# Sending each row of a GNN and mixture-of-experts kernel to its two experts, as 128 row tiles, in place of all eight experts over every row

## What is computed

```python
src, dst = (edge_index[0], edge_index[1])
h = jnp.einsum('ni,hid->nhd', x, W)
e = jnp.einsum('ehd,hd->eh', h_src, a_src) + jnp.einsum('ehd,hd->eh', h_dst, a_dst)
e = jnp.where(e > 0, e, 0.2 * e)
e_max = jax.ops.segment_max(e, dst, num_segments=N)
...
alpha_norm = alpha / (alpha_sum[dst] + 1e-08)
msg = alpha_norm[:, :, None] * h_src
out_h = jax.ops.segment_sum(msg, dst, num_segments=N)
return out_h.reshape(N, H * D) @ W_out
```

```python
logits = tokens.astype(jnp.float32) @ router_w.astype(jnp.float32).T
probs = jax.nn.softmax(logits, axis=-1)
rw, re = jax.lax.top_k(probs, TOP_K)
...
for e in range(E):
    h = jax.nn.gelu(tokens @ w1[e] + b1[e], approximate=False)
    y = h @ w2[e] + b2[e]
    out = out + combine[:, e:e + 1] * y
```

## Time and profile before

| | us |
|---|---|
| median of 3 runs | 1542.62 |
| the runs | 1541.4, 1542.62, 2022.45 |
| span of the profiled execution | 1540.1 |
| busy in it: TensorE, VectorE, ScalarE, POOL | 1407.5, 1098.5, 980.3, 835.1 |

### The profile page before, as it was taken

One profiled execution on the slowest core, in us unless ns is written; L12 is line 12 of the kernel. 1 busy time (PEld: TensorE's weight loads), 2 busy tenths in 40 slices (PEclk: granted clock), 3 DMA queues, 4 the chain that ended last, 5 costly groups with the idle time before them and its releaser, 6 DMA issues.

```text
span 1540.1 us, 29587 instructions
## 1 busy us (share of the span) xinstructions
PE 1407.5 (91%) x7327; PEld 1141.6 (74%) x7327; DVE 1098.5 (71%) x3031; ACT 980.3 (64%) x2505; POOL 835.1 (54%) x886
## 2 busy tenths in 40 slices
PE   5925775999999999999999999999999999999998
PEld 4813454788888888888888887878787878787887
DVE  6726765677777777777777787877777777777543
ACT  3714554576767676766667676767676767676732
POOL 1347777665666666565656565656565656561000
PEclk9966867799999999999999999999999999999999
DMA  9564654434343434343434343434434343473000
GB/s 221 145 193 121 193 146 118 128 99 124 107 126 105 125 104 125 104 120 111 117 112 118 114 117 113 117 111 115 114 106 124 102 129 99 133 90 59 1 17 18
DMA packets 89788, 174.83 MB, mean 114 GB/s; under 512 B 22455, under 2 KB 56049, under 8 KB 89593
## 3 DMA queue, kind: packets, MB, share of 16 engines
q0 software_dynamic: 40448, 111.89, 28.1%
q1 hardware_dynamic: 48071, 60.77, 13.2%
q10 hardware_dynamic: 1106, 0.27, 0.1%
HBM read 159.24 MB, written 14.43 MB: 113 GB/s over the span
## 4 chain that ended last, share of the span: by engine, by line
PE 74%; issue 6%; DVE 5%; POOL 4%; ACT 4%; ACTq 1%; DMA 1%; DVEq 0%; POOLq 0%
PE agg_ps L1117 24%; PE ob L1192 20%; PE hb L1146 15%; POOL ring L740 4%; PE kbank L1079 3%; PE ob L1223 2%; PE ob L1146 2%; PE ob L1258 2%; PE ob L1198 1%; ACT acc L1336 1%; DVE ring L848 1%; PE kbank L1095 1%; ACT agg_ps L1339 1%; PE kbank L1094 1%; DVE oh L785 1%
## 5 line engine op out<-in xcount | busy, mean ns | idle before, releaser
L740 POOL DMA_INDIRECT ring<-table,srcE x832 | 803.0, 965 | 504.3 <-PE agg_ps L1117 264.8
L1117 PE MATMUL agg_ps<-ring,oh 128*128 128x260 f32 x1664 | 550.9, 424 | 19.8 <-ACT agg_ps L1339 10.3
L1336 ACT COPY acc<-agg_ps x831 | 307.7, 370 | 188.1 <-PE agg_ps L1117 120.4
L1192 PE MATMUL ob<-w_sb,hT 128*125 128x256 f32 x1600 | 408.4, 380 | 1.6
L1339 ACT COPY agg_ps<-zc 128x260 f32 x832 | 314.6, 378 | 98.6 <-ACT acc L1336 3.2
L1117 PEld LDWEIGHTS agg_ps<-ring,oh 128*128 128x128 f32 x1664 | 292.2, 199 | 86.7 <-issue 55.2
L1192 PEld LDWEIGHTS ob<-w_sb,hT 128*125 128x125 f32 x1600 | 295.8, 188 | 52.7 <-issue 9.6
L848 DVE TENSOR_TENSOR ring<-ring,kbank 128x1024 f32<-128x1024 f32 x208 | 244.7, 1213 | 50.3 <-ACT ring L1358 50.1
L1368 ACT ACTIVATE hT<-hb,b_sb 128x375 f32<-128x375 f32 (+1 forms) x272 | 154.0, 566 | 146.0 <-PE hb L1146 145.1
L983 DVE SCALAR_TENSOR_TENSOR y<-ob,cmb,y 125x256 f32<-125x256 f32 x400 | 188.9, 475 | 46.7 <-PE ob L1192 43.1
L1146 PE MATMUL hb<-xTh,w1l 128*128 128x376 f32 (+1 forms) x544 | 186.3, 423 | 0.0
(11 more groups left out here) (271 smaller groups left out, 1376.8 us busy)
## 6 DMA issues: line engine op xcount, KB each, us to landing
OT<-relb_d SPq DMA_DIRECT2D x52, 512.0 KB
ring<-table,srcE POOLq DMA_INDIRECT x832
y<-in_x_dram SPq DMA_DIRECT2D x50, 125.0 KB
out_dram<-y SPq DMA_DIRECT2D x50, 125.0 KB
table<-hrow SPq DMA_DIRECT2D x25, 227.5 KB
acc<-in_x_dram SPq DMA_DIRECT2D x2, 1568.0 KB
acc<-in_L_ffn_w_dram SPq DMA_DIRECT2D x1, 2048.0 KB, 14.3
w_sb<-in_L_ffn_w_dram SPq DMA_DIRECT2D x1, 2048.0 KB
```

What stands on the lines that cost most here:

```text
L740: pool.indirect_dma_start(out=rings[b % RING][:, k, :], out_offset=None, in_=table[:, :], in_offset=bass.IndirectOffsetOnAxis(ap=srcE[:, t ...
L1117: T.matmul(aggf[:, bass.ds(bank_of[k // 8][k % 8], ROW)], oh[:, (4 * b + q) % OHQ, k % 4, :], rings[b % RING][:, k, :], start=False, stop= ...
L1192: t = T.matmul(o[0:Q, 0:D], hT[:, e % 2, f, cols], w2_sb[:, e, f, :], start=f == 0, stop=f == KC - 1)
L1336: A.copy(accf[:, bass.ds(row_of[h][k % 8], ROW)], aggf[:, bass.ds(closed[h][k % 8], ROW)]).then_inc(S["ev"], 1)
```

## The change

The dense loop over experts goes. In its place:

- VectorE finds in `differences` and `positions` where each row of a group goes among the rows of its two experts; TensorE counts for it with nine small bf16 products. POOL scatters each block's normalised rows twice to `xr_d` in DRAM (`scatter`, six indirect DMAs a group, at slot 43 of the 48).
- The groups form four super groups of 15, 15, 12 and 8 blocks. When one is complete, `tiles_table` (some 25 VectorE instructions) says which 128 rows and which expert each tile has; the tiles are 37, 37, 31 and 23, together 128.
- Tile n has a slot tau. SyncE loads its rows (`load_tile`) and its expert's first weights (`load_w1`). TensorE transposes the rows in slot tau (`turn_rows`), multiplies in tau + 2 (`hidden`) and tau + 4 (`output`), plain float32 products; ScalarE copies and does Gelu, VectorE adds the bias (`results_out`), SyncE stores to `yr_d`. The first super group's tiles lie at slots 310 to 543, the second's at 550 to 742, the third's at 748 to 887 and the fourth's, one in each slot, at 892 to 914. The edges end with slot 831. In a slot TensorE does the row tile's work ahead of the chain step and `aggregate`.
- After a super group's last tile POOL gathers the two results of each row, block by block (`results`, two indirect DMAs a block, 551 to 593, 750 to 792, 894 to 905 and 921 to 928), into a ring of two, and VectorE weighs and adds them (`final`).
- The router is six plain float32 products in place of 18; the split of w1 at the start goes.

The diff, cut:

```diff
+    SGS = [range(0, 5), range(5, 10), range(10, 14), range(14, GROUPS)]
+    NSG = len(SGS)
+    blocks_in = [sum(size(g) for g in r) for r in SGS]
+    CAP = [(-(-n * Q // P) + 1) * P for n in blocks_in]
+    NT = [(2 * n * Q + NE * (P - 1)) // P for n in blocks_in]
+    TMAX = max(NT)
...
+            RL, RW, RX, RH, RY, RR = 6, 4, 2, 3, 3, 2
...
+            LEAD = 12
+            sg_of = {g: s for s, r in enumerate(SGS) for g in r}
+            begin = [at(r[-1], 42) + LEAD for r in SGS]
+            first_tile = [sum(NT[0:s]) for s in range(NSG + 1)]
+            tau, sg_tile = [], []
+            for s in range(NSG):
+                for i in range(NT[s]):
+                    tau.append(begin[s] + (i * (begin[s + 1] - begin[s]) // NT[s] if s + 1 < NSG else i))
...
+                    result, final = (t + 8 + 3 * j, t + 14 + 3 * j) if s + 2 < NSG else (t + 7 + j, t + 9 + j)
...
+                    def fill_ends(s):
+                        sp.wait_ge(S["tb"], s + 1)
+                        for e in range(NE):
+                            end = loads(ENG.SP, emptyI[0:1, s, e:e + 1], BASE[NSG] - P, WHY2)[0]
+                            sp.dma_start(xr_d[bass.ds(end, P), :], zero_d[:, :]).then_inc(z_st[s], 16)
+
+                    def load_tile(n):
+                        s, i = sg_tile[n]
+                        r = n % RL
+                        if i == 0:
+                            fill_ends(s)
+                            for g in SGS[s][-2:]:
+                                sp.wait_ge(xs_st[g % 2], scattered(g))
+                            sp.wait_ge(z_st[s], 16 * (NE + 1))
+                        off = loads(ENG.SP, tileI[0:1, s, 0, i:i + 1], BASE[NSG] - P, WHY2)[0]
+                        if n >= RL:
+                            sp.wait_ge(S["xt"], n - RL + 1)
+                        sp.dma_start(rows[:, r, :], xr_d[bass.ds(off, P), :]).then_inc(row_ld[r], 16)
...
+                    def load_w1(n):
+                        s, i = sg_tile[n]
+                        if n == 0:
+                            sp.wait_ge(ld_w1, 32 * KC)
+                        expert = loads(ENG.SP, tileI[0:1, s, 1, i:i + 1], (NE - 1) * P, WHY2)[0]
+                        if n >= RW:
+                            sp.wait_ge(S["gl"], 2 * (n - RW + 1))
+                        sp.dma_start(w1s[:, n % RW, :], w1_d[bass.ds(expert, P), :]).then_inc(w1_ld[n % RW], 16)
...
+                    def store_tile(n):
+                        s, i = sg_tile[n]
+                        sp.wait_ge(S["ye"], n + 1)
+                        sp.dma_start(yr_d[s][i * P:(i + 1) * P, :], ysb[:, n % RY, :]).then_inc(yr_st[n % RY], 16)
...
+                    def scatter(g):
+                        u = g % 2
+                        pool.wait_ge(S["px"], g + 1)
+                        for i in range(size(g)):
+                            for k in range(2):
+                                pool.indirect_dma_start(out=xr_d[:, :], out_offset=bass.IndirectOffsetOnAxis(ap=idx[0:Q, block_at(g) + i, k:k + 1], axis=0),
+                                                        in_=xn[0:Q, u, i, :], in_offset=None).then_inc(xs_st[u], 16)
+
+                    def results(b):
+                        s = sg_of[b // GB]
+                        if b == block_at(SGS[s][0]):
+                            for r in range(RY):
+                                pool.wait_ge(yr_st[r], 16 * len(range(r, first_tile[s + 1], RY)))
+                        if b >= RR:
+                            pool.wait_ge(S["cb"], b - RR + 1)
+                        for k in range(2):
+                            pool.indirect_dma_start(out=res[0:Q, b % RR, k, :], out_offset=None, in_=yr_d[s][:, :],
+                                                    in_offset=bass.IndirectOffsetOnAxis(ap=idy[0:Q, b, k:k + 1], axis=0)).then_inc(res_ld[b % RR], 16)
+
+                    dev_at = {at(g, 20): g for g in range(GROUPS)}
+                    scatter_at = {at(g, 43): g for g in range(GROUPS)}
...
+                    for sl in range(-BT, LAST * BT):
+                        if sl in dev_at:
+                            deviations(dev_at[sl])
+                        if sl in scatter_at:
+                            scatter(scatter_at[sl])
+                        for b in result_at.get(sl, []):
+                            results(b)
+                        if sl % 4 == 3 and sl // BT + RING < NBAT:
+                            gathers(sl // BT + RING, sl % BT // 4)
...
-                    def split_x(g, part):
-                        u, blocks = g % 2, parts(g)[part]
-                        c0, n = blocks[0] * Q, len(blocks)
-                        dve.wait_ge(S["uh"], TC(g, part))
-                        cols = lambda a: a[:, u, :, c0:c0 + n * Q].rearrange("p k (b c) -> p b k c", c=Q)
-                        v.tensor_tensor(cols(xTl), ob1[:, 0:n * KC * Q].rearrange("p (b k c) -> p b k c", k=KC, c=Q), cols(xTh),
-                                        ALU.subtract).then_inc(S["ul"], 1)
...
+                    def positions(g):
+                        n, j0 = size(g), block_at(g)
+                        dve.wait_ge(S["ps"], g + 1)
+                        p_, o1, o2 = place_[0:Q, 0:n, :], one1[0:Q, 0:n, :], one2[0:Q, 0:n, :]
+                        link(v.tensor_tensor(p_, ob[0:Q, 0:n * NE].rearrange("p (b e) -> p b e", e=NE),
+                                             carry[0:Q, :].unsqueeze(1).to_broadcast([Q, n, NE]), ALU.add))
+                        pair_(v.tensor_tensor(at1[0:Q, 0:n, :], o1, p_, ALU.mult),
+                              v.tensor_tensor(at2[0:Q, 0:n, :], o2, p_, ALU.mult))
+                        pair_(v.tensor_reduce(spot[0:Q, j0:j0 + n, 0], at1[0:Q, 0:n, :], AX, ALU.add),
+                              v.tensor_reduce(spot[0:Q, j0:j0 + n, 1], at2[0:Q, 0:n, :], AX, ALU.add))
+                        link(v.tensor_tensor(carry[0:Q, :], ob[0:Q, 32:32 + NE], carry[0:Q, :], ALU.add))
+                        v.tensor_copy(idx[0:Q, j0:j0 + n, :], spot[0:Q, j0:j0 + n, :]).then_inc(S["px"], 1)
...
+                    def tiles_table(s):
+                        t, n2, j0 = NT[s], 2 * blocks_in[s], block_at(SGS[s][0])
+                        trash = float(BASE[s] + NE * CAP[s])
+                        cnt, til, tiI, cum, exl = (a[0:Q, :] for a in (cntE, tilE, tilI, cumE, exlE))
+                        link(v.tensor_tensor(cnt, carry[0:Q, :], regions[0:Q, s, :], ALU.subtract))
+                        link(v.tensor_scalar(tiI, cnt, float(P - 1), None, ALU.add))
+                        link(v.tensor_scalar(tiI, tiI, 7, None, ALU.arith_shift_right))
+                        link(v.tensor_copy(til, tiI))
...
-                    def accumulate(g, e, i):
-                        u = g % 2
-                        o = ob0 if i != 1 else ob1
...
+                    def results_out(n):
+                        s, i = sg_tile[n]
+                        if n == 0:
+                            dve.wait_ge(ld_b2, 16)
+                        dve.wait_ge(S["y2"], n + 1)
+                        if n >= RY:
+                            dve.wait_ge(yr_st[n % RY], 16 * (n // RY))
+                        v.tensor_tensor(ysb[:, n % RY, :], ybank[:, 0:D], b2_sb[:, bass.ds(bias_of[s, i // 8][i % 8], D)],
+                                        ALU.add).then_inc(S["ye"], 1)
+
+                    def final(b):
+                        a, r = acc[0:Q, b, 0:D], b % RR
+                        dve.wait_ge(res_ld[r], 32 * (b // RR + 1))
+                        dve.wait_ge(S["yi"], b // GB + 1)
+                        link(v.scalar_tensor_tensor(a, res[0:Q, r, 0, :], wt[0:Q, b, 0:1], a, ALU.mult, ALU.add))
+                        v.scalar_tensor_tensor(a, res[0:Q, r, 1, :], wt[0:Q, b, 1:2], a, ALU.mult, ALU.add).then_inc(S["cb"], 1)
...
-                    def exact(out_, lhs, rhs):
-                        terms = [(lo, hi2) for (_, lo), (hi2, _) in zip(lhs, rhs)]
-                        terms += [(hi, lo2) for (hi, _), (_, lo2) in zip(lhs, rhs)]
-                        terms += [(hi, hi2) for (hi, _), (hi2, _) in zip(lhs, rhs)]
-                        for j, (a, b_) in enumerate(terms):
-                            t = T.matmul(out_, a, b_, start=j == 0, stop=j == len(terms) - 1)
-                        return t
-
-                    def hidden(g, e, f):
...
-                        exact(hbank[f][:, 0:w], [(w1h[:, e, k, fs], w1l[:, e, k, fs]) for k in range(KC)],
-                              [(xTh[:, u, k, 0:w], xTl[:, u, k, 0:w]) for k in range(KC)]).then_inc(S["h1"], 1)
...
-                                t = exact(ob1[0:Q, i * NE:(i + 1) * NE], [(xTh[:, u, k, cols], xTl[:, u, k, cols]) for k in range(KC)],
-                                          [(rwh[:, k, :], rwl[:, k, :]) for k in range(KC)])
+                                for k in range(KC):
```

(52 more changed lines are left out.)

503 lines of the change are left out of this document (237 added, 266 removed).

## The result

The changed kernel takes 1720.1 us (1715.6 to 1725.6 in four runs) against 1542.0, a ratio of 1.116 with an interval of 1.113 to 1.119. One of the four runs of the kernel before, at 2022 us, was in a slower state and is not in the ratio. Slower was right. The time is 118 us over the forecast of 1602 and 45 over the upper end of the range.

What follows compares the result with a forecast made beforehand. It took TensorE as the bound before the change, then the slower of POOL's list and the chain of edges. 258.6 + 1134 + 207 = 1600 us of span, so a median of 1602 us; range 1530 to 1675.

Steps and rivals of the forecast that it cites:

- What bounds it now, and POOL as the expert-free pace: TensorE paces the kernel before; without experts POOL's list does, at 1.253 us per indirect DMA, 68.9 us per 48 slots.
- the signs put down: Expected if right: roots 69 us apart, 73 after slot 310, 81 to 94 at first results; POOL idle below 5%.
- The chain without tiles, 66.0: The chain of edges with no expert tiles takes 66.0 us per 48 slots, below POOL's 68.9.
- No row shows a scatter into DRAM: POOL's scatters priced like the ring's gathers, 1.253 us each, with ends of 1.0 and 1.6.
- The table load of 1.28: ScalarE's table load, once more per batch beside tiles, delays messages by some 0.8 us: +2.4 per 48 slots.
- Results, +49: Where results fall, POOL's extra DMAs add 8, 21 and 6 us, and the last `final` on VectorE 14: +49.
- The tail, 207: From the root of group 15 to the end 207 us, against 102.5 before: +104.5; bounds 160 and 245.
- Rival A: The chain hides the tiles and keeps POOL's pace: part 1 at 1083, 1551 us in all; chance 0.22.
- Rival B: The chain hides the tiles at POOL's pace, and a tail without gaps takes 160: 1504 us; chance 0.08.
- Rival C: TensorE's clock falls, half the time at half clock, and the tail takes 245: 1692 us; chance 0.08.
- Rival D: SyncE's `load_tile` waits for scatters, delaying the next fetch; chain stops 20 us at three borders: 1662 us; chance 0.07.
- slower of the two rules: Between roots of groups 0 and 15, the slower of POOL's list and the chain sets each stretch: 1134 us.

Runs made afterwards that it cites:

- e4: Kernel before the change with 18 small indirect DMAs added on POOL after each group's root; 1647.2 us, ratio 1.069.
- e11: Changed kernel without scatters, gathers of results and the waits on them, a tile's rows read from a fixed place; 1600.4 us, ratio 1.040.
- e16: Kernel of e11 with the exponential in place of Gelu, so no table loads between the two; 1557.4 us, ratio 1.012.
- e15: Kernel of e11 with two of four first products and one of two outputs per tile left out; 1570.1 us, ratio 1.018.
- e1: Changed kernel without the gathers of results on POOL and VectorE's wait for their landing; 1634.9 us, ratio 1.061.
- e2: Changed kernel with one unread 128 x 256 filler product per slot on TensorE from slot 80, except around tile turns; 1762.0 us, ratio 1.144.
- e17: Changed kernel with later stores, spread results, sooner loads, and the first three super groups' tiles 10 slots later, fills left in place; 1658.5 us, ratio 1.076.
- e3: Changed kernel with the first three super groups' tiles, and their loads, 12 slots later; 1715.5 us, ratio 1.113.
- e14: Changed kernel with the exponential in place of Gelu, so ScalarE keeps one table; 1681.3 us, ratio 1.091.
- e5: Same kernel as e11, on a slower chip where the kernel before took 1710.5 us; 1823.5 us.
- e6: Changed kernel with first weights loaded for four tiles only, on a slower chip where the kernel before took 1710.5 us; 1991.7 us.
- e12: Same kernel as e6, first weights loaded for four tiles only, on a normal chip; 1705.1 us, ratio 1.105.
- e8: Changed kernel with the first two super groups' result gathers starting later and every 4 slots, on the slower chip; 1997.7 us.

## Why the prediction came out as it did

- *What bounds it now, and POOL as the expert-free pace.* Right. e4 shows the rule by itself (84 to 85 for 83.9), e11 shows that with a shorter list the same slots take 64.8. Of the signs put down, roots 69 apart came as 70.5 to 71.6, 73 with tiles as 74.2 to 78.7, and 81 to 94 at the first results as 98.9 and 104.3; POOL's idle share in part 1 was 10%, not below 5.
- *The chain without tiles, 66.0.* Right to 1.2 us (64.8, e11), in part by luck: of its small terms the -3 was for a full clock, and e11 was granted 0.76 there.
- *"No row shows a scatter into DRAM; it is the same instruction with 125 rows in place of 128, and I take 1.253 (ends: 1.0 and 1.6)".* Wrong, and carried on to the results without a word. The scatters cost 1.50 and the results 1.54. That is 23 + 17 us on POOL's list in part 1, less 8 by which gathers and roots were cheaper: 1115 in place of 1083. The first stretch shows it bare, 284.1 against 275.6: 6 of these 8.5 us are its 24 scatters.
- *"The table load of 1.28, once more per batch than in the free stretch, delays messages by some 0.8: +2.4."* The 0.8 was right (0.79, e16), the number was not: 7 loads per 48 slots, not 3. A Gelu between two exponentials costs two loads, one to its table and one back, and the view of before from which the forecast took its 12 loads between 700 and 1000 us, of ScalarE's exponentials, had 12 more for Gelu:

```profile
L1368 ACT ACT_TABLE_LOAD x12 | 15.4, 1283 | 0.2
```

So tiles cost 1.46 us each in e11, not 0.85: 0.74 for tables, 0.17 to 0.24 for half of the products (e15; the forecast had 0.14 for all), and the rest is near the 0.42 put down for `results_out`, which was not tested alone.
- *Results, +49.* Of the right order (e1, without the sums: 40 to 47 in part 1, for 35). That 8, 21, 6 and 14 were read at places of their own was wrong in the second: the stretch is POOL's list at its true prices, 104.3, not 94.0.
- *The tail, 207.* Right to 5% (217.7), while the loss of 104 was 115. In part that is luck, since the terms missed both ways: the first of the last tiles was turned 90 us behind the root of group 15 (1585.93) and not 99, with a hand-over of 0.15 among the terms that no row shows, and the results cost 3.5 to 3.8 a block, not 2.83: each pair takes 3.0 on POOL, and in front of most second blocks POOL waited 0.6 to 2.4 us for a sum of the block two before. Three of these rows:

```profile
1687.56 1.21 POOL L870 DMA_INDIRECT res<-yr_d,idy  x1 [0.30 <-issue]
1690.12 1.21 POOL L870 DMA_INDIRECT res<-yr_d,idy  x1 [1.35 <-DVE acc L1177]
1691.64 1.21 POOL L870 DMA_INDIRECT res<-yr_d,idy  x1 [0.30 <-issue]
```

- *Rival A* (POOL's floor, 1551) is out: at POOL's true prices its sum is 32 higher, so 1583, and with tiles the roots stood 75.5 apart where POOL's list by itself had kept 71.0 without them, so the chain did not hide the tiles. *Rival B* falls with it, and by a tail of 217.7 for its 160. *Rival C* is out as a cause: the clock did fall (mean 0.818; the runs of the kernel before beside e1 had 0.955), but where POOL sets the pace e2 lifted it and gained nothing, with tiles it was 0.91 and 0.96 for C's 0.75, and in e15 TensorE has less to do at 0.783 and the kernel is no slower.
- *Rival D, "SyncE's list stops the edges".* It had 0.07 and a price of 20 us at three borders. It is the nearest to what the forecast's sum lacked. I had looked for it in the fetch behind `load_tile`'s waits for the scatters; it is in front of them: SyncE stood 537 us in all at its batches' fetches and 388 at the tiles' stores, then writes eight fills in 7.5 us, and TensorE has the tile's turn at the head of its list with the chain behind it, for 13.7, 10.6 and 8.7 us. e17 takes 61 us out of part 1 (1237.6 to 1176.6) by lists alone; that D's three borders make 60 is luck, since these three waits are 33, and e3 shows that a wait taken away need not be time won.

So the steps that failed are two, which together are the 104 us by which part 1 was too short. One is the price of an indirect DMA that no row of before showed, taken from its cheapest neighbour and not from the upper bound that was worked out beside it (32 us on POOL's floor). The other is the "slower of the two rules" by which part 1 was summed, which let every engine meet its next instruction at once. In the changed kernel POOL's list of 1115 had 123 us of waits on top; the sum had 51 over its 1083. Waits on SyncE's and POOL's lists (e17: 61) and table loads in front of the chain (e14: 30 in part 1) overlap and don't add up: they are 91 for the 72 us by which the waits were too small. The table loads are also a term of the sum that was mis-sized: 5.5 us per 48 slots where 2.4 was taken.

Not settled: the 714 to 810 stretch keeps 176 to 178 us in e11 and e16, with no gather of results and in e16 no table load, against 150 to 164 for 102 slots just before. Tiles are denser there (10.0 in 48 slots), and a border lies in it; this was not tried apart.

## What to carry to other kernels

Work that is taken off the fullest engine does not come back as time when it is replaced by hand-overs: here TensorE's busy time fell by 19 us in 100, and waits between the engines and lists that issue DMAs took their place. Price such a list by itself, every instruction at the price of its own shape, and then ask at each place where an engine's in-order list has a wait at its head what stands behind it: a first tile that waits for rows behind eight fills stops the chain that needs no rows. When single moves of waits give little, move them together once before the theory is dropped (here 57 us, where the parts that were run had given 9 and 7), and then run the missing part alone, which was not done here. And a rearrangement that ends work in a tail (this one's 115 us) has to win that much in the middle before it is even.

## What the runs showed of the hardware that I had not expected

- An indirect DMA of 125 rows of 1,024 bytes holds POOL longer than one of 128 rows of 1,040: 1,204 ns (scatter into DRAM) and 1,240 (gather from DRAM) against 969 for the ring. Small ones of 4 bytes a row (e4) took 0.95, as the ring's. The size is not what decides; why 125 rows cost more was not tried.
- The same programs took 11% (the kernel before), 14% (e5 against e11) and 17% (e6 against e12) longer on one chip than on the others. The instructions did not take longer (in e8 the ring's gather 969 ns and the one-hot 684, in the changed kernel 968 and 683); the waits between them were.
- Half of TensorE's products for the tiles were worth 1.3 to 1.8 us in 48 slots, and ScalarE's seven table loads, which compute nothing, 5.5.
